# Layer 2's item (2, 6) split into high and low parts by halves in a PSUM bank, in an embedding tower on one core

## The chip, the core and the metric

The kernel runs on one core of a Trainium2 chip. The metric is the device time of one execution in microseconds, from the runs listed below. TensorE is called PE in the rows, its weight loads PEld, VectorE DVE, ScalarE ACT, GpSimd POOL and SyncE SP.

## What is computed

32 embedding tables are looked up for 1024 samples (16 numbers each), and a network of three layers works on the outcome, where each layer multiplies every field of x with every row of the last hidden state and sums with weights:

```python
for i in range(3):
    z = (x0[:, :, None, :] * h[:, None, :, :]).reshape(B, F * G, E)     # F = 32, G = 32 or 64
    y = relu(einsum('oc,bce->boe', Ws[i], z) + bs[i][None, :, None])    # 128 outputs
    x_keep, h = (y[:, :64], y[:, 64:]) if i != 2 else (y, y)
    xs.append(x_keep)
z = sum(concatenate(xs, axis=1), axis=2)
h = relu(concatenate([z, dense_ctx], axis=1) @ W_top1 + b_top1)
return relu(h @ W_top2 + b_top2) @ W_top3
```

All of it is float32. A product of a weight and an activation is made either with one float32 matmul of both (a "whole" item), or with three matmuls of a rounded type, float32r, on high and low parts: high weight by high product, low weight by high product, high weight by low product (a "split" item).

## The kernel before

**Tiles and items.** The batch has 8 blocks of 128 samples, and each block 4 tiles of 4 embedding places, so 32 tiles of 512 columns. A layer's products for one tile are cut into chunks of 128 rows, and two chunks make an item (layer, n): layer 0 has 2 items and a tail, layers 1 and 2 have 8 each. An item takes VectorE one multiplication of 128x1024 numbers (L1070): a slice of `spread` or `shifted` (the fields' rows, copied to all lanes by DMA) by the hidden state, which lies in a PSUM bank (`xT`, `h0` or `h1`).

**Slots.** The order of all work is one list written by hand (SLOT, L78), which all engines follow, each in its own order of instructions. A slot handles layer 1 of tile n, layer 2 of tile n - 1 and layer 0 of tile n + 1:

```python
SLOT = [(1, 0), (1, 1), (2, 0), (1, 2), (2, 1), (1, 3), (0, 0), (2, 2), TAIL, (1, 4), (0, 1),
        (2, 3), (1, 5), (2, 4), (1, 6), (2, 5), (1, 7), (2, 6), (2, 7)]
```

There are 34 slots, from -1 to 32. Slots 2 and up lie in a hardware loop, four to a round. The last slot has layer 2 alone.

**Whole items.** Layers 0 and 1 and item (2, 6) are whole (L101). Their products go into `prod`, a ring of 4 buffers, so VectorE waits with a product until TensorE has used the one four whole items earlier (L1067). TensorE multiplies them by w0T, w1T or w2T_whole: two chunks, each as two instructions of a float32 matmul, so four in the rows (L617).

**Split items.** The other seven of layer 2 go through three engines: VectorE writes the product (`unsplit`), ScalarE copies it to the rounded type (`high`, L829), GpSimd subtracts it from the product (`low`, L500) in the place of the product. TensorE runs four matmuls of the high part (L625) in the item's place in the list, and the two of the low part (L640) one item later. In the last slot items (2, 2), (2, 5) and (2, 7) are subtracted by VectorE (L1078).

**GpSimd.** Between its subtractions it issues the look-ups of the next block, 8 to a slot (LOOKUPS_AFTER, L95): in three slots of four one ahead of the first subtraction, then 0, 0, 1, 1, 1, 2, 2 after the seven. Of each four slots one begins a block (`begin`, L483 to L487): it waits until all look-ups of the block before have landed (s_looked) and ScalarE has copied them to `emb` (L793), takes the new indices (ids_now, L477), and goes on to look up (L490). In that slot the numbers are 0, then 0, 0, 2, 0, 1, 2, 3. The last two look-ups of a block come after the subtraction of (2, 7). ScalarE's copy to `emb` stands after its high part of (2, 2) in the slot that begins, ahead of the tail's two copies, and GpSimd's subtraction of the tail (L508) stands ahead of `begin`. Look-ups for the last block are out after slot 25, and then GpSimd only subtracts.

**ScalarE.** Besides the high parts it makes, once a slot: `next_h0` (L831), which takes layer 0's second half from y0 to the hidden state of the next tile and its first half to `kept` (three activations, after item (2, 4), as soon as TensorE has used (0, 1)); `take_x` (L805), a copy of transposed x out of xT, after (2, 5), which waits for TensorE's transposes `turn_x` (L581, L589) after (2, 4) in its own order; and, at the slot's end, `h1` (L815, L880) and the second `kept`, when TensorE has used (1, 7). The next slot's (1, 0) on TensorE waits for that `kept` (begin_layer, L601), and VectorE's (1, 0) for h0, its (2, 0) for h1. h0 has two banks, which alternate by tile.

**VectorE** also adds the kept rows (L1101; L1097 is its first in a block, a copy) after (1, 1), adds layer 2's outcome (L1114, L1109), and folds both once a block (L1120).

**SyncE** issues the loads of a slot in order: x out to HBM when take_x is done (L394), the shifted rows and four loads of 1 MB of `spread` (L416), each when VectorE has made the last product that reads the old ones: (2, 1), (2, 3), (2, 5), (2, 7).

After the last tile comes a small dense network (`three_passes`), its first layer in between the items of the last slot.

## Time and profile before

| what | value |
|---|---|
| median of 3 runs | 1061.19 us |
| the three runs | 1063.73, 1061.14, 1061.19 us |
| the profiled execution's own time | 1066.62 us |
| its span, first to last instruction | 1064.8 us |
| mean granted clock of TensorE | 0.976 |
| TensorE busy | 94% |
| VectorE busy | 77% |
| GpSimd busy | 77% |
| ScalarE busy | 45% |
| 16 DMA engines, mean rate | 174 GB/s |

The profiled execution took 5.4 us longer than the median. The rows come from it. A busy share of TensorE contains modelled ends of matmuls. The idle time in brackets at a row is that of its engine just before it, with what ended it; "issue" means that the profile shows nothing that was waited for. Weight loads run one matmul ahead of their matmul.

### The profile page before, as it was taken

The numbers are of one execution on the slowest core, as the hardware profiler recorded it, in microseconds if no ns is written. First come the engines' busy times: TensorE is split into PE (matmuls) and PEld (weight loads), VectorE is DVE, ScalarE is ACT, GpSimd is POOL, SyncE is SP. The second block draws the span as 40 slices with busy tenths as digits, with TensorE's granted clock in tenths as the row PEclk, the third lists the DMA queues.
The fourth block names the chain that finished last, engine by engine and source line by source line (L and its number), as shares of the span: only waits on it lengthen the run. The fifth ranks groups of instructions, "written<-read, shape, count | busy, mean of one in ns | idle before, by whom it ended". The sixth has DMA issues, their size and how long they took to land.

```text
span 1064.8 us, 11324 instructions
## 1 busy us (share of the span) xinstructions
PE 995.8 (94%) x3089; PEld 572.8 (54%) x3089; DVE 821.8 (77%) x750; ACT 474.4 (45%) x595; POOL 816.3 (77%) x524
## 2 busy tenths in 40 slices
PE   3178899999999999999999999999899999999988
PEld 2133455555555555555555555555455555555565
DVE  6234877798778977899778977898778977788882
ACT  2222544444544454454444454444444454543443
POOL 7655779887998879887998789886998766566540
PEclk9579999999999999999999999999999999999989
DMA  8089999989888888899888888888888888889000
GB/s 158 10 189 198 205 199 190 210 191 197 191 194 191 191 192 185 192 198 208 191 194 186 194 188 190 187 192 191 195 187 188 192 186 192 190 186 219 30 1 0
DMA packets 49012, 185.45 MB, mean 174 GB/s; under 512 B 17570, under 2 KB 22178, under 8 KB 28388
## 3 DMA queue, kind: packets, MB, share of 16 engines
q1 hardware_dynamic: 40804, 183.15, 78.2%
q0 software_dynamic: 8192, 2.11, 2.0%
q8 instruction: 7, 0.11, 0.0%
q14 instruction: 9, 0.07, 0.0%
HBM read 182.06 MB, written 3.15 MB: 174 GB/s over the span
## 4 chain that ended last, share of the span: by engine, by line
POOL 42%; PE 26%; issue 18%; DMA 7%; DVE 4%; ACT 2%; SPq 0%; POOLq 0%; ACTq 0%; DVEq 0%
POOL low L500 24%; POOL looked_up L490 16%; PE y L617 15%; PE y L625 6%; DMA looked_up<-in_tbl,ids_now 4%; PE y L640 3%; POOL tail_parts L508 2%; DMA spread<-xcols 2%; DVE unsplit L1070 1%; DVE prod L1070 1%; DMA xcols<-xrows 0%; ACT emb L793 0%; ACT tail_high L853 0%; PE y L721 0%; DVE acc_kept L1101 0%
## 5 line engine op out<-in xcount | busy, mean ns | idle before, releaser
L500 POOL TENSOR_TENSOR low<-unsplit,high 128x1024 fp32r<-128x1024 f32 x221 | 525.1, 2388 | 113.3 <-ACT high L829 111.5
L617 PE MATMUL y<-prod,w1T 128*128 128x512 f32 x1024 | 480.3, 597 | 5.4 <-ACT kept L821 2.7
L1070 DVE TENSOR_TENSOR prod<-spread,h 128x1024 f32<-128x1024 f32 x288 | 349.1, 1216 | 118.3 <-PE y L617 102.6
L829 ACT CAST high<-unsplit 128x1024 fp32r<-128x1024 f32 x224 | 234.0, 1045 | 243.6 <-DVE unsplit L1070 243.2
L1070 DVE TENSOR_TENSOR unsplit<-spread,h 128x1024 f32<-128x1024 f32 x224 | 272.1, 1215 | 48.8 <-ACT h L815 48.6
L490 POOL DMA_INDIRECT looked_up<-in_tbl,ids_now x256 | 248.7, 971 | 69.1 <-issue 59.4
L617 PEld LDWEIGHTS y<-prod,w1T 128*128 128x128 f32 x1024 | 193.5, 192 | 166.8 <-issue 144.1
L625 PE MATMUL y<-high,w2T_high 128*128 128x512 f32 x448 | 226.7, 506 | 4.4 <-ACT high L829 4.4
L640 PE MATMUL y<-low,w2T_high 128*128 128x512 f32 x448 | 202.7, 533 | 6.3 <-POOL low L500 6.3
L625 PE MATMUL y<-high,w2T_low 128*128 128x512 f32 x448 | 177.9, 397 | 0.0
L815 ACT ACTIVATE h<-y,bias 64x512 f32<-64x512 f32 x128 | 83.3, 651 | 209.2 <-PE y L617 208.3
L640 PEld LDWEIGHTS y<-low,w2T_high 128*128 128x128 f32 x448 | 84.4, 191 | 91.3 <-issue 61.5
L617 PE MATMUL y<-prod,w0T 128*128 128x512 f32 x256 | 122.2, 600 | 5.5 <-DVE prod L1070 5.5
L625 PEld LDWEIGHTS y<-high,w2T_high 128*128 128x128 f32 x448 | 84.9, 190 | 50.0 <-issue 29.4
L625 PEld LDWEIGHTS y<-high,w2T_low 128*128 128x128 f32 x448 | 84.9, 190 | 43.4 <-issue 29.0
L1070 DVE TENSOR_TENSOR prod<-shifted,xT 128x1024 f32<-128x1024 f32 x64 | 77.7, 1215 | 22.8 <-DMA shifted<-xcols 15.4
L617 PEld LDWEIGHTS y<-prod,w0T 128*128 128x128 f32 x256 | 48.9, 192 | 49.3 <-issue 45.0
L508 POOL TENSOR_TENSOR tail_parts<-tail,tail_high 128x512 fp32r<-128x512 f32 x32 | 41.0, 1283 | 25.7 <-ACT tail_high L853 25.6
L617 PE MATMUL y<-prod,w2T_whole 128*128 128x512 f32 x128 | 60.1, 592 | 0.0
L821 ACT ACTIVATE kept<-y,bias_kept 64x512 f32<-64x512 f32 x64 | 43.7, 682 | 1.6
L809 ACT COPY xrows<-xT 48x512 f32<-48x512 f32 x32 | 18.5, 579 | 50.6 <-PE xT L589 50.6
L589 PE MATMUL xT<-ident,four_times 128*128 128x128 f32 x128 | 20.2, 282 | 22.2 <-ACT four_times L801 22.2
(115 smaller groups left out, 441.3 us busy)
## 6 DMA issues: line engine op xcount, KB each, us to landing
spread<-xcols SPq DMA_DIRECT2D x128, 1024.0 KB, 9.0
shifted<-xcols SPq DMA_DIRECT2D x124, 256.0 KB
shifted_tail<-xcols SPq DMA_DIRECT2D x124, 64.0 KB
looked_up<-in_tbl,ids_now POOLq DMA_INDIRECT x256
xcols<-xrows SPq DMA_DIRECT2D x32, 96.0 KB, 2.0
spread<-in_L_rec_W SPq DMA_DIRECT2D x3, 512.0 KB, 7.0
spread<-in_L_rec_W SPq DMA_DIRECT2D x1, 1024.0 KB, 11.6
wt<-in_W_top SPq DMA_DIRECT2D x2, 512.0 KB, 8.7
```

What stands on the lines that cost most here:

```text
L490: pool.indirect_dma_start(out=looked_up[:, f, :], out_offset=None, in_=tables[f][:, :], in_offset=bass.IndirectOffsetOnAxis(ap=ids_now[:, ...
L500: pool.tensor_tensor(low[kind][r][:, :, :], unsplit[kind][r][:, :, :], high[kind][r][:, :, :].bitcast(F32), ALU.subtract).then_inc(s_low[k ...
L508: pool.tensor_tensor(tail_parts[:, :], tail[:, :], tail_high[:, :].bitcast(F32), ALU.subtract).then_inc(s_tail_low, 1)
L589: last = pe.transpose(xT[:, P * e:P * (e + 1)], four_times[:, e, :, :].rearrange("p a f -> p (a f)"), ident[:, :])
L617: last = pe.matmul(y[:, :], w, z[:, c, :], start=(n == 0 and c == 0), stop=(item in (LAST0, LAST1) and c == ITEM - 1))
L625: pe.matmul(y[:, :], w[:, ITEM * n + c, :], z[:, c, :], start=(n == 0 and c == 0 and w is w2T_high), stop=False)
L640: last = pe.matmul(accumulator(s, layer)[:, :], w2T_high[:, ITEM * n + c, :], z[:, c, :], start=False, stop=(item == LAST2 and c == ITEM - 1))
L809: act.copy(xrows[:, :], xT[0:XROWS, :]).then_inc(s_xrows, 1)
L815: last = act.activation(h[to, :], y[lanes, :], ACT.Relu, bias=bias[lanes, :])
L821: act.activation(kept[t[1] % KEPT][lanes, :], y[lanes, :], ACT.Relu, bias=bias_kept[lanes, :]).then_inc(s_kept, 1)
L829: act.copy(high[kind][r][:, :, :], unsplit[kind][r][:, :, :]).then_inc(s_high[kind], 1)
L1070: dve.tensor_tensor(z, x[:, ITEM * n:ITEM * (n + 1), :], b[:, :].unsqueeze(1).to_broadcast([P, ITEM, COLS]), ALU.mult).then_inc(s_made[kin ...
```

## The change

Item (2, 6) is no longer whole. In the last slot it is split like the others, with GpSimd's subtraction, and the order there is as before. In all other slots that have layer 2 it is split with VectorE's, chunk by chunk in one PSUM bank, `part`, and without a place in `unsplit`: VectorE writes the product of a chunk to the bank (`make_part`), ScalarE copies it from there to the high part (`part_high`), VectorE subtracts the high part from the bank into the low part (`part_low`), and only then makes the second chunk there. The bank is taken from h0, which has one bank instead of two, so `next_h0` also waits until VectorE has made (1, 7), the last product that reads the old h0, and moves from behind (2, 4) to behind (1, 7) in ScalarE's order. VectorE and ScalarE follow a new list with the last items in another order (MADE), while TensorE, GpSimd and SyncE keep SLOT. The ring `prod` keeps 4 buffers and holds ten items a slot instead of eleven. `w2T_whole` and its copy are gone.

```diff
+MADE = SLOT[:-4] + [(2, 6), (2, 5), (1, 7), (2, 7)]
-WHOLE2 = (2, 6)
+IN_PARTS = (2, 6)
 def kind_of(item, last):
-    if item[0] < 2 or item == WHOLE2:
+    if item[0] < 2:
         return WHOLE
-    return BY_DVE if last and item in LAST_BY_DVE else BY_POOL
+    return BY_DVE if item in (LAST_BY_DVE if last else [IN_PARTS]) else BY_POOL
+def made_items(items):
+    return [x for x in MADE if x in items] if IN_PARTS in items and (1, 7) in items else items
-        w2T_whole = sb("w2T_whole", [P, ITEM, P])
-        h0 = [ps(f"h0_{p}", [P, COLS]) for p in range(2)]
+        h0 = ps("h0", [P, COLS])
+        part = ps("part", [P, COLS])
...
+            def part_high(s, c):
+                e = plan.entry(s, IN_PARTS)
+                act.wait_ge((s_part, s_made[BY_DVE])[c], e + 1)
+                to = high[BY_DVE][plan.place(s, IN_PARTS, RING)]
+                act.copy(to[:, c, :], part[:, :]).then_inc((s_part_high, s_high[BY_DVE])[c], 1)
             def next_h0(s):
                 act.wait_ge(s_used[WHOLE], plan.entry(s, LAST0) + 1)
-                go_on(h0[(s[1] + 1) % 2], y0, 1, bias0, s_h0)
+                if LAST1 in plan.items(s):
+                    act.wait_ge(s_made[WHOLE], plan.entry(s, LAST1) + 1)
+                go_on(h0, y0, 1, bias0, s_h0)
...
-                h0_after = (2, 4) if (2, 4) in items else None
+                h0_after = (1, 7) if (2, 4) in items else None
-                for item in items:
+                last_slot = plan.is_last(s)
+                for item in made_items(items):
...
+                    elif item == IN_PARTS and not last_slot:
+                        part_high(s, 0)
                     elif plan.kind(s, item) != WHOLE:
+                        if item == LAST2 and not last_slot:
+                            part_high(s, 1)
                         split_high(s, item)
...
-                    if WHOLE2[1] // (GROUP // ITEM) == n - 2 - GROUPS:
-                        of = ITEM * WHOLE2[1] % GROUP
-                        dve.tensor_copy(w2T_whole[:, :, :], source[:, of:of + ITEM, :])
...
+            def make_part(s, c):
+                e = plan.entry(s, IN_PARTS)
+                if c == 0 and (not isinstance(e, int) or e >= RING[BY_DVE]):
+                    dve.wait_ge(s_used[BY_DVE], e - RING[BY_DVE] + 1)
+                if c == 1:
+                    dve.wait_ge(s_part_low, e + 1)
+                elif not isinstance(e, int) or e >= 1:
+                    dve.wait_ge(s_low[BY_DVE], e)
+                dve.tensor_tensor(part[:, :], spread[(s[1] - 1) % 2][:, ITEM * IN_PARTS[1] + c, :], h1[:, :],
+                                  ALU.mult).then_inc((s_part, s_made[BY_DVE])[c], 1)
+            def part_low(s, c):
+                e = plan.entry(s, IN_PARTS)
+                dve.wait_ge((s_part_high, s_high[BY_DVE])[c], e + 1)
+                r = plan.place(s, IN_PARTS, RING)
+                dve.tensor_tensor(low[BY_DVE][r][:, c, :], part[:, :], high[BY_DVE][r][:, c, :].bitcast(F32),
+                                  ALU.subtract).then_inc((s_part_low, s_low[BY_DVE])[c], 1)
...
             def slot(s):
                 waiting = None
                 items = plan.items(s)
-                for item in items:
-                    mine = item != TAIL and plan.kind(s, item) == BY_DVE
-                    multiply(s, item)
-
+                in_parts = IN_PARTS in items and not plan.is_last(s)
+                for item in made_items(items):
+                    whole_item = not (in_parts and item == IN_PARTS)
+                    mine = item != TAIL and whole_item and plan.kind(s, item) == BY_DVE
+                    if whole_item:
+                        multiply(s, item)
+                    else:
+                        make_part(s, 0)
+
+                    if in_parts and item == (2, 5):
+                        part_low(s, 0)
+                    if in_parts and item == LAST1:
+                        make_part(s, 1)
+                    if in_parts and item == LAST2:
+                        part_low(s, 1)
```

## Rows read from the trace of the kernel before

**Rows 1.** Page, busy us (share of the span) xinstructions of three engines

```profile
PE 995.8 (94%) x3089; PEld 572.8 (54%) x3089; DVE 821.8 (77%) x750; ACT 474.4 (45%) x595; POOL 816.3 (77%) x524
```

**Rows 2.** Busy time by stretch: us, PE, PEld, DVE, ACT, POOL, PEclk, DMA share, GB/s

```profile
200.00:900.00 700.00, 696.70 (x2160) 399.06 (x2159) 579.22 (x509) 331.08 (x409) 591.46 (x369) 1.00 0.88 192
```

**Rows 3.** Timeline of weight loads, slots at 573 and 602, and one late load

```profile
573.13 0.42 PEld L617 LDWEIGHTS y<-prod,w1T 128*128 128x128 f32 x2
579.01 0.19 PEld L640 LDWEIGHTS y<-low,w2T_high 128*128 128x128 f32 x1 [0.24 <-issue]
602.45 0.42 PEld L617 LDWEIGHTS y<-prod,w1T 128*128 128x128 f32 x2
...
520.68 0.30 PEld L640 LDWEIGHTS y<-low,w2T_high 128*128 128x128 f32 x2 [1.00 <-POOL low L500]
```

**Rows 4.** Page, chain of work that ended last, share of the span by engine

```profile
POOL 42%; PE 26%; issue 18%; DMA 7%; DVE 4%; ACT 2%; SPq 0%; POOLq 0%; ACTq 0%; DVEq 0%
```

**Rows 5.** Chain of work late on: start us, us, what; items (2, 6) and (2, 7)

```profile
955.78 1.72 PE y L617 x4
957.50 0.93 PE y L625 x4
```

**Rows 6.** Timeline of VectorE, slot that starts at 573.13

```profile
568.00 3.38 DVE L1101 TENSOR_TENSOR acc_kept<-acc_kept,kept 128x512 f32<-128x512 f32 x1
...
579.19 0.67 DVE L1052 TENSOR_TENSOR tail<-shifted_tail,xT 128x512 f32<-128x512 f32 x1
579.79 1.21 DVE L1070 TENSOR_TENSOR prod<-spread,h 128x1024 f32<-128x1024 f32 x1
...
588.20 1.21 DVE L1070 TENSOR_TENSOR unsplit<-spread,h 128x1024 f32<-128x1024 f32 x1
...
597.32 3.12 DVE L1097 COPY acc_kept<-kept 128x512 f32<-128x512 f32 x1
```

**Rows 7.** Timeline of GpSimd: start us, us, engine, line, operation [idle before]

```profile
510.99 2.36 POOL L500 TENSOR_TENSOR low<-unsplit,high 128x1024 fp32r<-128x1024 f32 x1
518.24 7.06 POOL L500 TENSOR_TENSOR low<-unsplit,high 128x1024 fp32r<-128x1024 f32 x3
...
593.03 2.38 POOL L500 TENSOR_TENSOR low<-unsplit,high 128x1024 fp32r<-128x1024 f32 x1 [1.59 <-ACT high L829]
597.77 2.37 POOL L500 TENSOR_TENSOR low<-unsplit,high 128x1024 fp32r<-128x1024 f32 x1
614.60 0.21 POOL L477 COPY ids_now<-ids_sb 128x32 int32 x1
```

**Rows 8.** Timeline of ScalarE in the slot that starts at 573.13

```profile
589.99 1.32 ACT L815 ACTIVATE h<-y,bias 64x512 f32<-64x512 f32 x2 [2.73 <-PE y L617]
591.91 1.03 ACT L829 CAST high<-unsplit 128x1024 fp32r<-128x1024 f32 x1
594.54 0.58 ACT L809 COPY xrows<-xT 48x512 f32<-48x512 f32 x1 [1.59 <-PE xT L589]
595.02 1.04 ACT L829 CAST high<-unsplit 128x1024 fp32r<-128x1024 f32 x1
599.30 1.31 ACT L815 ACTIVATE h<-y,bias 64x512 f32<-64x512 f32 x2 [3.24 <-PE y L617]
```

**Rows 9.** Chain of work in the middle: start us, us, what

```profile
497.04 0.22 POOL ids_now L477
...
601.58 8.66 DMA looked_up<-in_tbl,ids_now
```

**Rows 10.** Waits of the weight loads up to 200 us: us in total, times, longest

```profile
PEld xT L589 <- ACT four_times L801: 22.6, 1, 22.6
```

**Rows 11.** Timeline of GpSimd where its loop of slots ends

```profile
744.01 0.96 POOL L490 DMA_INDIRECT looked_up<-in_tbl,ids_now  x1 [3.80 <-issue]
```

**Rows 12.** Timeline of VectorE in the last slot

```profile
1026.71 2.43 DVE L1147 TENSOR_TENSOR z_kept_low<-z_kept,z_high 128x512 fp32r<-128x512 f32 x1
1031.34 0.68 DVE L1155 TENSOR_TENSOR hidden_low<-hidden,hidden_high 128x512 fp32r<-128x512 f32 x1
```

13 lines of the change are left out of this document (8 added, 5 removed).

## The prediction

> **What bounds the kernel now.** I read the page's busy times first: TensorE is at 94% of the span, VectorE and GpSimd at 77% each [rows 1]. The table by stretch sharpens that: from 200 to 900 us TensorE is busy for 696.7 of 700 us at the full granted clock [rows 2]. The weight loads give the period of a slot: item (1, 0) starts at 573.13 and again at 602.45, so 29.32 us [rows 3]. So TensorE's own work sets the pace, and a shorter item shortens the slot. But the page's chain of work that ended last runs through GpSimd for 42% of the span and through TensorE for 26% [rows 4]. That is the warning: in each block there is a long unbroken run of GpSimd, and its end shows at one weight load, which comes 1.00 us after the last in place of the usual 0.24, waiting for a low part [rows 3]. GpSimd is barely in time there.
>
> I write A for the slot that starts at 573.13, B for the next (602.45), C for the one after, and "A+20" for a time 20 us into A.
>
> **TensorE's gain.** The whole item is four instructions in 1.72 us, the four of a split item's high part 0.93 us, so 0.2325 each [rows 5]. Split, (2, 6) takes six: 6 x 0.2325 = 1.40. Gain 0.32 us a slot, 29.32 to 29.00, in 32 slots at most 10.2 us (1.0%). The Trainium skill, "TensorE: Matmul & The Clock Gate", Back-to-back issue gap, gives 131 ns for a matmul of 512 columns in a stream with weight loads. By it six take 0.79 us and the gain would be 0.93 a slot; the trace has 232 ns, and the measurement decides.
>
> **VectorE's added work.** One multiplication of 128x1024 goes and four operations of 128x512 come. The tail's product, with one operand in PSUM, is such a one: 0.67 us, the next starts after 0.60 [rows 6]. A 1024 multiplication has 1.21 us, so by the same overlap a pitch of about 1.13. So 4 x 0.60 - 1.13 = +1.3 us a slot. No row has VectorE writing PSUM. I take the tail's 0.60; the bounds are 0.3 less (half the tail's) and that of the worst VectorE row of this size, 3.38 us [rows 6]. VectorE is busy for 579.2 of 700 us [rows 2], so idle for 5.1 us in a slot, and its time itself is hidden. If that cover were gone, 1.3 us a slot would be 42 us. `part_low` reads one operand from PSUM, and this decides whether it meets GpSimd: additions with both operands in SBUF take 0.68 alone [rows 12] and 3.38 or, a copy, 3.12 us when a GpSimd subtraction runs [rows 6, 7], while multiplications from PSUM keep 1.21 beside it. The Trainium skill, "SBUF — State Buffer", Who interferes with whom, says a VectorE instruction with at most one SBUF input does not contend with GpSimd; by it `part_low` stays at 0.6, and from two SBUF operands it would be up to 3. The trace agrees for multiplications; no row has a subtraction of this kind.
>
> **ScalarE's order is the costly part.** Before, `next_h0` ran at A+16.9 (589.99), between the high parts of (2, 4) and (2, 5); then (2, 5) at 591.91, `take_x` at 594.54, which waits for TensorE's transposes, then (2, 7) at 595.02 [rows 8]. Now `take_x` comes before `next_h0`, which stands behind (1, 7). So after A+21.4, ScalarE does in one run: take_x 0.48, h0 1.34, kept 0.58, second half of (2, 6) about 0.5 (take_x's own pitch), high part of (2, 7) 1.05. Done at A+25.4, before A+22.9. Three things stand behind it:
> - h1 starts at A+26.2 (599.30) when (1, 7) is done, as before [rows 8]; 0.7 us are left.
> - VectorE's second `part_low` is at A+24.4, and behind it in VectorE's order (1, 0), (1, 1), the addition and (2, 0). (1, 0) is made at A+26.2, needed at A+29.0. The addition falls on A+27.3, onto GpSimd's low part of (2, 7), and ends about A+28.5; (2, 0) is made at A+29.7 and its high part at 30.8. TensorE wants it after (1, 0) and (1, 1), at A+29.0+3.4=32.4. Hidden, with 1.6 us left. In A, which has two folds, VectorE ran from 571.4 (568.00 + 3.38, A-1.7) without a pause; now it starts at about A-0.2, so it makes (2, 5) from A+17.2 in place of A+15.1 (588.20) plus the first half [rows 6]; (1, 7) at A+20.2 is before A+21.9, where h0 needs it.
> - GpSimd's low part of (2, 7). It started at A+24.64 (597.77), after the two look-ups behind (2, 5) (593.03) [rows 7]. Now it can't before A+25.5: **+0.85 us**.
>
> **What that 0.85 meets.** Behind that low part come a block's last two look-ups; the last lands and reaches ScalarE 8.66 us after it is issued [rows 9], then emb, the tail and the new block's indices at B+12.15 (614.60) [rows 7]. Relative to B this moves by 0.85 + 0.32 to B+13.3. From there GpSimd has no pause: from the like point of the block before, 497.04, it ends the low part of (2, 7) at 513.35 (16.3 later) and of the next (2, 0) at 520.6 (23.6 later) [rows 7, 9]. Now:
> - (2, 7)'s low part ends at B+29.6. TensorE wants it 0.47 us before the slot's end, with its load 0.23 earlier at most, B+28.5: stall 1.1 us.
> - (2, 0)'s, at B+36.9. C starts at B+30.1, wants it at C+5.88 (579.01 - 573.13) [rows 3], B+36.0; a load runs some 0.3 ahead there, so 0.6 more.
> Before, the same sum gives 35.8 + 0 against 29.32 + 5.88 = 35.2, less 0.3: a stall of 0.3, which is the late load of the rows. So a block of four slots takes 4 x 29.32 + 0.3 = 117.6 now (614.60 - 497.04 = 117.56 [rows 7, 9]) and 4 x 29.00 + 1.7 = 117.7 after. **GpSimd's run takes back the gain** in the six blocks' time in which look-ups are issued: 6 x 0.15 = +0.9 us. The stall of 3.80 us in one issue where GpSimd's loop ends [rows 11] stays as it is; it is in the same run.
>
> **Without look-ups**, from about 780 us on, nine items (2, 6) gain in full: -2.9 us.
>
> **Start.** w2T_whole's copy goes from VectorE's preparation: TensorE's first transposes wait 22.6 us for the first look-ups after that [rows 10], so 0. ScalarE's `next_h0` in slot 0 may wait for (1, 7): up to +0.5, taken as 0.
>
> **End.** Slot 31 has VectorE in one run with extra subtractions of the dense network, so the added 1.3 us are not fully hidden; in the last slot the item's low part comes to GpSimd at 1031.4, where VectorE has a subtraction out of SBUF at 1031.34 that takes 0.68 [rows 12], and such a one takes 2.43 when it meets GpSimd. Bounds: -0.3 (the PE time alone) and 1.3 + 1.75 = +3.0; I take +1.0, below the middle, since TensorE still has a unit of the dense layer to do meanwhile.
>
> **Sum.** 0.9 - 2.9 + 0 + 1.0 = -1.0 us on the profiled execution's own 1066.6 (span 1064.8 and 1.8 around it): 1065.6. The median stands 5.4 lower, so 1060.2. A measurement tells about 0.3% (3.2 us) from no change.
>
> **Rivals.**
> 1. *GpSimd has more room than the profile shows; the gain comes through.* For: the timed runs are 5.4 us shorter, and TensorE's work can't be what shrank from 200 to 900 us, so part of that may be GpSimd's issue and the look-ups' landing. If the run of 40 us from (2, 7)'s low part in A to (2, 0)'s in C is 1.7 us shorter, no stall is left: -10.2 + 0.3 x 6 for what the faster run of before also saves there, + 1.0 at the end: about -8, 1053. At half of it, 1057. Against: GpSimd's subtractions have 2.36 to 2.38 us wherever they stand [rows 7], so they show no disturbance.
> 2. *The last look-up lands later: slower.* The DMA engines are at 88% [rows 2]; SyncE's megabyte loads are issued at the same time as a block's last two look-ups, and these now come 0.85 us later among them. Each microsecond beyond 8.66 goes into the run uncovered, six times. It decides from 0.7 us on: six times 0.7 - 1.0 = +3.2. With 1.5 us: +8, 1069. Against: the megabyte loads are out in any case by then, and a look-up is small beside them.
> 3. *VectorE and ScalarE take turns badly.* A write to the bank at twice the tail's time, or a wait of each of the four steps of 0.1 us, moves (2, 7)'s high part, thus +0.5 a block and 0 elsewhere: +3, 1064.
> 4. *The change does not do what it says:* accesses of `part` beside TensorE's banks hold TensorE, or the six matmuls don't run at 0.2325. Nothing in the rows is for it: 1061 to 1064.
>
> **Chances.** Forecast 45%; rival 1, 35%; rival 2, 10%; rivals 3 and 4, 5% each. Faster by over 0.3%: 0.36 (rival 1 and a little of the forecast); same 0.47; slower 0.17. The range takes in the forecast with its end at both bounds (1059 to 1063), rival 1 whole, and the near part of 2 and 3: 1052.5 to 1065.5.
>
> **What the changed profile would show.** Distance of (1, 0)s 29.00 where nothing waits; TensorE's gaps before (2, 7)'s and (2, 0)'s low part of 1.1 and 0.6 us in one slot pair of four; `next_h0` at A+21.9 and (2, 7)'s high part ending at A+25.4; `part` operations on VectorE of about 0.67. Wrong would be: those gaps gone while GpSimd's indices are at B+13.3 or sooner; high parts later than A+26; TensorE waiting for (2, 0)'s high part or for ScalarE's kept.

## The result, and the profile after

| what | before | after |
|---|---|---|
| median | 1063.73 us of 7 | 1054.62 us of 7 |
| range | 1061.14 to 1065.91 | 1053.63 to 1056.56 |
| profiled execution's own time | 1066.62 | 1055.05 |
| its span | 1064.8 | 1053.2 |

The ratio is 0.9925 [0.9913, 0.9938]: faster by 0.75%, 8.0 us. (The two medians of the table are 9.1 us apart; the ratio with its interval is the figure used here.) The forecast was 1060.2, 1.0 us below the kernel before, and "within 0.3%" as its likeliest case. What came is close to rival 1, the gain comes through, with its 1053. The difference of the two profiled spans, 11.6 us, is larger than the ratio says: before's profiled execution took longer than any of its seven timed ones.

Page of the changed kernel, busy times and the chain that ended last:

```profile
PE 987.6 (94%) x3153; PEld 585.1 (56%) x3153; DVE 829.3 (79%) x842; ACT 511.2 (49%) x658; POOL 823.2 (78%) x525
PE 61%; POOL 17%; issue 8%; DMA 5%; DVE 5%; ACT 2%; SPq 0%; POOLq 0%; DVEq 0%; ACTq 0%
```

Against [rows 1], TensorE has 64 matmuls more (each whole item had four, a split one has six) and 8.2 us less to do. VectorE has 92 instructions more and 7.5 us more busy time, ScalarE 63 and 36.8 us. The chain, which ran through GpSimd for 42% and TensorE for 26% [rows 4], now has 17% and 61%. Most of what GpSimd held in it is TensorE's now.

Table by stretch, 200 to 900 us, columns as in [rows 2]:

```profile
200.00:900.00 700.00, 698.21 (x2234) 412.94 (x2233) 587.72 (x590) 363.40 (x463) 601.71 (x373) 1.00 0.89 195
```

TensorE rose from 696.7 to 698.2 of 700 us at the full granted clock, though each slot has less work for it: waits have gone, not come. The forecast wanted the opposite, 1.7 us of wait in four slots in place of 0.3, so some 8 us less than before in this stretch (six blocks by 1.4).

Timeline of weight loads, start of slots A (568.27) and B (597.30), the transposes of `turn_x` in A (588.75), and the one late load in the slot after B:

```profile
568.27 0.43 PEld L627 LDWEIGHTS y<-prod,w1T 128*128 128x128 f32 x2
588.75 0.38 PEld L599 LDWEIGHTS xT<-ident,four_times 128*128 128x128 f32 x2
597.30 0.42 PEld L627 LDWEIGHTS y<-prod,w1T 128*128 128x128 f32 x2
632.81 0.30 PEld L650 LDWEIGHTS y<-low,w2T_high 128*128 128x128 f32 x2 [0.86 <-POOL low L510]
```

From 568.27 to 597.30 are 29.03 us, and over many slots 29.01: the 29.00 of the forecast. Of the two late loads that it wanted in each block there is one, before the low part of (2, 0), with 0.86 us in place of the usual 0.24. It makes that slot 29.33, by 0.32 longer than the others. Before, the same load came late as well [rows 3], and the slot was longer by 0.29 to 0.45.

Timeline of ScalarE over the end of A and the start of B:

```profile
589.69 0.58 ACT L819 COPY xrows<-xT 48x512 f32<-48x512 f32 x1 [2.31 <-PE xT L599]
590.30 1.32 ACT L825 ACTIVATE h<-y,bias 64x512 f32<-64x512 f32 x2
591.64 0.69 ACT L831 ACTIVATE kept<-y,bias_kept 64x512 f32<-64x512 f32 x1
592.22 0.57 ACT L846 CAST high<-part 128x512 fp32r<-128x512 f32 x1
592.69 1.05 ACT L839 CAST high<-unsplit 128x1024 fp32r<-128x1024 f32 x1
594.45 1.31 ACT L825 ACTIVATE h<-y,bias 64x512 f32<-64x512 f32 x2 [0.72 <-PE y L627]
603.32 1.05 ACT L839 CAST high<-unsplit 128x1024 fp32r<-128x1024 f32 x1 [2.35 <-DVE unsplit L1091]
604.27 0.61 ACT L803 COPY emb<-looked_up 128x512 f32<-128x512 f32 x1
```

This is the order that the forecast worked out: `take_x` at A+21.4 (589.69 - 568.27 = 21.42), h0 at A+22.0 where A+21.9 was forecast, part_high 0.57 where 0.5 was, and the high part of (2, 7) done at A+25.47 where A+25.4 was. The last two rows are what was not worked out. `emb` is copied at 604.27 right behind the high part of (2, 2), which had waited for VectorE's product; there is no wait for a DMA. Before, ScalarE was done with that high part and then waited 1.5 us for the look-ups.

Timeline of GpSimd from (2, 7)'s low part in A to the three subtractions ahead of the late load:

```profile
593.82 2.40 POOL L510 TENSOR_TENSOR low<-unsplit,high 128x1024 fp32r<-128x1024 f32 x1 [1.31 <-ACT high L839]
596.36 0.97 POOL L500 DMA_INDIRECT looked_up<-in_tbl,ids_now  x1
597.63 0.94 POOL L500 DMA_INDIRECT looked_up<-in_tbl,ids_now  x1 [0.31 <-issue]
...
608.62 0.21 POOL L487 COPY ids_now<-ids_sb 128x32 int32 x1
...
622.83 2.39 POOL L510 TENSOR_TENSOR low<-unsplit,high 128x1024 fp32r<-128x1024 f32 x1 [0.32 <-ACT high L839]
...
630.37 4.76 POOL L510 TENSOR_TENSOR low<-unsplit,high 128x1024 fp32r<-128x1024 f32 x2
```

(2, 7)'s low part starts at A+25.55, where "not before A+25.5" was forecast; the step of +0.85 us is there, and the row names ScalarE's high part as what ended 1.31 us of idle time. But the new indices (608.62) are at B+11.32. The forecast had B+13.3; before it was B+12.15 [rows 7]. This is where the forecast and the chip part.

Timeline of VectorE in A, then the groups of the two new operations (min/median/max in ns):

```profile
592.82 0.69 DVE L1112 TENSOR_TENSOR low<-part,high 128x512 fp32r<-128x512 f32 x1 [3.08 <-ACT high L846]
593.53 2.35 DVE L1091 TENSOR_TENSOR prod<-spread,h 128x1024 f32<-128x1024 f32 x2
595.80 0.70 DVE L1139 COPY acc_kept<-kept 128x512 f32<-128x512 f32 x1
596.42 1.21 DVE L1091 TENSOR_TENSOR unsplit<-spread,h 128x1024 f32<-128x1024 f32 x1
L1104 DVE TENSOR_TENSOR part<-spread,h x62: 675/683/690, 116.8 to 996.1; 128x512 f32<-128x512 f32 x62
L1112 DVE TENSOR_TENSOR low<-part,high x62: 672/684/693, 118.5 to 997.8; 128x512 fp32r<-128x512 f32 x62
```

The operations in `part` take 0.683 and 0.684 us (0.67 forecast), and in 62 cases each never over 0.693, whether the bank is the destination or an operand. A subtraction of GpSimd runs beside 60 of the products and beside 23 of VectorE's subtractions, and none of these is over 0.690. The copy of the kept rows took 3.12 us on top of GpSimd's low part before [rows 6]. The forecast had it at A+27.3, on the end of that low part, and done at about A+28.5. It starts at A+27.53 with 0.4 us of GpSimd's subtraction still to go (593.82 + 2.40 = 596.22) and takes 0.70.

The Trainium skill, "SBUF — State Buffer", Who interferes with whom, says that a VectorE instruction with at most one input in SBUF, outside the two-port modes, does not contend with GpSimd. The trace agrees for `part_low` too (at most 0.683 us in the 23 beside a GpSimd subtraction), which the trace of before could not show.

Waits from 200 to 900 us, us in total, times, longest:

```profile
PEld y L650 <- POOL low L510: 6.4, 6, 1.5
DVE low L1112 <- ACT high L846: 111.4, 24, 5.4
ACT xrows L819 <- PE xT L599: 93.3, 24, 4.6
ACT emb L803 <- DMA looked_up<-in_tbl,ids_now: 0.5, 1, 0.5
```

TensorE's waits for a low part were 16.7 us in the same view of before, 42 times; 6.4 us in 6 waits are left. VectorE idles for 111.4 us before the subtraction of a half, all of it hidden. ScalarE's wait for a looked-up row was 8.8 us, six times, up to 1.7; it is 0.5, once.

**Where the time went**, by the distances between the transposes from slot 3 to slot 31 in the two profiled executions. Before: 28 slots of 29.32 are 821.0 us, and 7.7 more in stalls. After: 28 of 29.01 are 812.3, and 5.2 in stalls. So TensorE's shorter slot gives 8.7 us, and stalls 2.5. All of the 2.5 is one place, the slot in which GpSimd's loop ends: 33.25 us before (3.9 over), 30.35 after (1.3 over). There GpSimd pauses ahead of one look-up, for 3.80 us before [rows 11] and 1.48 after. From the last slot's transposes to the end it is 115.1 before and 114.6 after, where the forecast added 1.0.

### The profile page after: what moved, and what is told of

Read it like the earlier page. It is cut to its first block, busy times and chain, and to the rows that moved or that the text cites. A ratio compares the mean times of both kernels' runs of the same rounds, so it can differ in the third digit from the quotient of the medians.

```text
span 1053.2 us, 11585 instructions
## 1 busy us (share of the span) xinstructions
PE 987.6 (94%) x3153; PEld 585.1 (56%) x3153; DVE 829.3 (79%) x842; ACT 511.2 (49%) x658; POOL 823.2 (78%) x525
## 4 chain that ended last, share of the span: by engine, by line
PE 61%; POOL 17%; issue 8%; DMA 5%; DVE 5%; ACT 2%; SPq 0%; POOLq 0%; DVEq 0%; ACTq 0%
PE y L627 36%; PE y L635 15%; POOL looked_up L500 8%; POOL low L510 8%; PE y L650 8%; DMA xcols<-xrows 2%; DMA shifted<-xcols 2%; DVE unsplit L1091 2%; DVE prod L1091 1%; PE xT L599 1%; DMA looked_up<-in_tbl,ids_now 1%; PE y L644 1%; SPq L411 0%; POOL tail_parts L518 0%; ACT h L825 0%
## 5 line engine op out<-in xcount | busy, mean ns | idle before, releaser
L1091 DVE TENSOR_TENSOR prod<-spread,h 128x1024 f32<-128x1024 f32 x256 | 306.6, 1209 | 16.0 <-ACT h L825 9.6
L635 PE MATMUL y<-high,w2T_high 128*128 128x512 f32 x512 | 240.3, 469 | 4.6 <-ACT high L839 4.6
L650 PE MATMUL y<-low,w2T_high 128*128 128x512 f32 x512 | 218.5, 516 | 3.1 <-POOL low L510 2.8
L635 PE MATMUL y<-high,w2T_low 128*128 128x512 f32 x512 | 203.0, 396 | 0.0
L1112 DVE TENSOR_TENSOR low<-part,high 128x512 fp32r<-128x512 f32 x62 | 42.5, 685 | 133.0 <-ACT high L846 133.0
L650 PEld LDWEIGHTS y<-low,w2T_high 128*128 128x128 f32 x512 | 96.3, 190 | 90.6 <-issue 71.3
L635 PEld LDWEIGHTS y<-high,w2T_high 128*128 128x128 f32 x512 | 96.9, 189 | 47.5 <-issue 19.6
L635 PEld LDWEIGHTS y<-high,w2T_low 128*128 128x128 f32 x512 | 96.7, 189 | 40.6 <-issue 22.0
L1091 DVE TENSOR_TENSOR prod<-shifted,xT 128x1024 f32<-128x1024 f32 x64 | 77.4, 1209 | 17.1 <-DMA shifted<-xcols 15.9
L518 POOL TENSOR_TENSOR tail_parts<-tail,tail_high 128x512 fp32r<-128x512 f32 x32 | 41.0, 1280 | 15.9 <-ACT tail_high L873 15.9
L846 ACT CAST high<-part 128x512 fp32r<-128x512 f32 x62 | 35.8, 577 | 33.9 <-DVE part L1104 33.9
```

Source lines behind the costliest of these rows:

```text
L518: pool.tensor_tensor(tail_parts[:, :], tail[:, :], tail_high[:, :].bitcast(F32), ALU.subtract).then_inc(s_tail_low, 1)
L635: pe.matmul(y[:, :], w[:, ITEM * n + c, :], z[:, c, :], start=(n == 0 and c == 0 and w is w2T_high), stop=False)
L650: last = pe.matmul(accumulator(s, layer)[:, :], w2T_high[:, ITEM * n + c, :], z[:, c, :], start=False, stop=(item == LAST2 and c == ITEM - 1))
L846: act.copy(to[:, c, :], part[:, :]).then_inc((s_part_high, s_high[BY_DVE])[c], 1)
L1091: dve.tensor_tensor(z, x[:, ITEM * n:ITEM * (n + 1), :], b[:, :].unsqueeze(1).to_broadcast([P, ITEM, COLS]), ALU.mult).then_inc(s_made[kin ...
L1112: dve.tensor_tensor(low[BY_DVE][r][:, c, :], part[:, :], high[BY_DVE][r][:, c, :].bitcast(F32), ALU.subtract).then_inc((s_part_low, s_low[ ...
```

## Why the indices come earlier

The forecast took over the 8.66 us from a block's last look-up to `emb` [rows 9]. In the changed kernel it is 604.27 - 597.63 = 6.64, and in the blocks before and after it 6.63. These 6.6 us are not the look-up's own time: ScalarE has no wait for it there, so they only tell when ScalarE gets to `emb`, B+6.97, where it was B+7.81 before. The packets of the look-ups' queue tell when the look-ups landed. I compare two stretches of 4 us in each kernel, from 9 to 13 us behind the transposes (which are at 588.75 after and 593.6 before) and from 13 to 17. DMA view of the changed kernel, 597.7 to 601.7 us (in the next stretch it has none):

```profile
q0 software_dynamic: 64, 0.02, 2.3%
```

The same of the kernel before, 602.6 to 606.6 and 606.6 to 610.6 us:

```profile
q0 software_dynamic: 32, 0.01, 1.2%
q0 software_dynamic: 32, 0.01, 1.8%
```

Each look-up is 32 packets. Before, the last two land one by one, the second in the later stretch; after, both land in the first, in spite of being issued 0.9 us later against the transposes. SyncE's issues, changed kernel first:

```profile
586.32 0.54 SPq L426 DMA_DIRECT2D spread<-xcols  x1
590.48 0.36 SPq L404 DMA_DIRECT2D xcols<-xrows  x1
593.86 1.87 SPq L411 DMA_DIRECT2D shifted<-xcols  x4
598.02 2.44 SPq L426 DMA_DIRECT2D spread<-xcols  x2
```

and before:

```profile
589.43 0.54 SPq L416 DMA_DIRECT2D spread<-xcols  x1
595.33 0.36 SPq L394 DMA_DIRECT2D xcols<-xrows  x1
597.32 1.88 SPq L401 DMA_DIRECT2D shifted<-xcols  x4
601.48 15.96 SPq L416 DMA_DIRECT2D spread<-xcols  x4
```

Both kernels write x out 1.7 us behind the transposes. The load ahead of it, the third megabyte of `spread`, is issued 4.2 us before them in the old kernel and 2.4 in the new one, since VectorE now makes the first half of (2, 6) ahead of (2, 5), and that load waits for (2, 5). x's way out queues behind it: the shifted rows, which wait for x, go out at +3.7 before and +5.1 after, and the next megabyte at +7.9 and +9.3. So the two look-ups (at +6.7 and +8.0 before, +7.6 and +8.9 after) now are both issued ahead of that megabyte; before, the second came behind it. How much that order is worth can be read from all 14 traces of this case, the experiments below among them, in five blocks of each (those whose `emb` comes after 250 us): how long behind the last look-up SyncE issues the next megabyte, and how long behind it the look-up's last packet is done.

| next megabyte issued | blocks | last packet done |
|---|---|---|
| from 0.5 us ahead of the last look-up to 0.17 behind it | 24 | 5.85 to 8.0 us behind the look-up |
| 0.21 us or more behind the last look-up | 46 | 3.35 to 5.3 us behind the look-up |

No block is an exception, and several kernels have blocks in both rows. The changed kernel has one in the first, at 371.79 (0.16 us, done after 6.3, a wait of 0.5), and so has its repetition e11, here in a timeline of GpSimd, SyncE (716 to 719 us) and ScalarE:

```profile
717.10 0.94 POOL L500 DMA_INDIRECT looked_up<-in_tbl,ids_now  x1 [0.30 <-issue]
717.13 0.58 SPq L426 DMA_DIRECT2D spread<-xcols  x1
725.54 0.62 ACT L803 COPY emb<-looked_up 128x512 f32<-128x512 f32 x1 [1.72 <-DMA looked_up<-in_tbl,ids_now]
```

The megabyte is 0.03 us behind the look-up there, the packets are done after 7.65, and `emb` comes 8.44 us behind it, as in the kernel before. So a look-up issued 0.2 us or more ahead of the megabyte lands some 3 us sooner. What follows for `emb` is less than these 3 us, because ScalarE's high part of (2, 2) then comes last: it is at most the wait for the look-up, 1.5 us in the block shown.

## The experiments

Each ran beside the kernel before on the same chip, and ratios are to that one. This table puts together what the weight loads and GpSimd's index copies of each profile say: a slot's distance where nothing waits, how much longer the slot with the late load is in the blocks of slots 12 to 23, and the place of the new indices behind the start of slot B (slot 20, or the one a block earlier).

| kernel | ratio | slot | stall per block | indices | in the loop's last slot |
|---|---|---|---|---|---|
| before | 1 | 29.32 | 0.29, 0.45, 0.29 | 12.15 | 3.9 |
| after | 0.9925 | 29.01 | 0.64, 0.32, 0.32 | 11.3 | 1.3 |
| e11, the same again | 0.9931 | 29.01 | 0.32, 0.32, 0.33 | 11.3 | 1.9 |
| e1 | 0.9996 | 29.31 | 0 | 11.7 | 1.7 |
| e2 | 1.0021 | 29.32 | 0.6, 0.7, 0.6 | 12.2 | 4.4 |
| e3 | 1.0025 | 29.01 | 2.4, 2.4, 2.4 | 12.9 | 6.0 |
| e4 | 1.0057 | 29.49 | 0.3, 0.5, 0.1 | 11.9 | 0.8 |
| e5 | 0.9935 | 29.01 | 0.4, 0.9, 0.4 | 11.4 | 2.2 |
| e6 | 0.9932 | 29.01 | 0.41, 0.37, 0.40 | 11.3 | 1.6 |
| e7 | 0.9850 | 28.55 | 1.5, 1.4, 1.1 | 12.0 | 3.1 |
| e8 | 0.9905 | 29.01 | 0.1, 0, 0 | 10.8 | 1.3 |
| e9 | 1.0000 | 29.01 | 2.1, 2.1, 2.1 | 12.6 | 3.6 |
| e10 | 1.0002 | 29.01 | 1.6, 1.5, 1.6 | 11.4 (first of five) | 6.7 |
| e12, e8 again | 0.9912 | 29.01 | 0.1, 0, 0 | 11.0 | 1.7 |

### e1: only the third load, later (kernel before)

```diff
-                    item = (2, GROUP // ITEM * (g + 1) - 1)
+                    item = WHOLE2 if g == 2 else (2, GROUP // ITEM * (g + 1) - 1)
```

> The kernel before, with one thing changed: SyncE issues the third of the four loads of spread in a slot when VectorE has made (2, 6), not (2, 5), about 1.8 us later. Theory L (the block's last look-up lands sooner in the changed kernel because the third load, now issued later, pushes x's way out to HBM and the fourth load back, so that the last two look-ups are served ahead of that load): the last look-up reaches ScalarE 7 us or less after its issue in place of 8.7, the new block's indices come about 1.5 us earlier in the slot, the late low part once a block (0.3 us) goes, and the time falls by 1 to 4 us. Rival (the look-ups land sooner because they are issued 0.9 us later themselves): landing stays 8.7 us, the time is that of before within 0.1%.

1062.93 us, ratio 0.9996 [0.9985, 1.0007]: no change. The stall of 0.3 us in a block is gone, and the look-ups' packets have all moved by 12.5 us behind the transposes (12.2 to 12.9 in four of the changed kernel's five blocks, 15.1 to 15.9 before). So moving the third load alone, and with it the next, makes the look-ups land sooner. But `emb` comes at 8.2 to 8.5 us behind the last look-up all the same, where 7 or less was expected; that expectation failed. VectorE's waits show why:

```profile
DVE prod L1070 <- DMA shifted<-xcols: 16.9, 21, 2.6
```

In this kernel VectorE is there before the shifted rows and waits for them, 21 times, so the high part of (2, 2), behind which ScalarE has `emb`, comes later itself. In the changed kernel VectorE has that wait once, for 0.7 us. So the early landing isn't enough: it takes effect in the changed kernel because VectorE there hardly waits for those rows. And with TensorE's old slot there were only the 0.3 us a block to be had, which is below what the comparison can tell.

### e2: only ScalarE's order and the one bank (kernel before)

```diff
-        h0 = [ps(f"h0_{p}", [P, COLS]) for p in range(2)]
+        h0 = ps("h0", [P, COLS])
...
+                if LAST1 in plan.items(s):
+                    act.wait_ge(s_made[WHOLE], plan.entry(s, LAST1) + 1)
+                go_on(h0, y0, 1, bias0, s_h0)
...
-                h0_after = (2, 4) if (2, 4) in items else None
+                h0_after = (1, 7) if (2, 4) in items else None
```

> The kernel before with one bank for h0 and next_h0 behind (1, 7), item (2, 6) whole as before. Theory T (only TensorE's shorter item gives time): the slot stays 29.32 us where nothing waits, the time is that of before within 0.3%; the high part of (2, 7) ends at A+24.9, the low part of (2, 7) starts there instead of at A+24.6. Rival (the single bank and the order cost something that the shorter item hides in the changed kernel): 0.3% or more slower, by the look-ups' run: up to six times 1 us. A second rival (the order itself gives part of the gain, by better turns of the DMA queues): faster by 1 to 3 us.

1065.43, ratio 1.0021 [1.0012, 1.0029]. The order with the single bank costs 2.2 us, with stalls of 0.6 to 0.8 a block. Here the last look-up still takes 8.4 to 8.7 us to `emb`, so the later high part is handed on as the forecast said. The next megabyte is issued ahead of the last look-up in all five blocks, by 0.05 to 0.5 us.

### e3: the item split, with its product in SBUF as one piece (kernel before)

```diff
-    if item[0] < 2 or item == WHOLE2:
+    if item[0] < 2:
         return WHOLE
-    return BY_DVE if last and item in LAST_BY_DVE else BY_POOL
+    return BY_DVE if item in (LAST_BY_DVE if last else [WHOLE2]) else BY_POOL
```

(and `w2T_whole` left out).

> The kernel before, with (2, 6) split by VectorE in the ordinary way: product of 128x1024 to SBUF, high part by ScalarE, subtraction out of SBUF by VectorE; two banks for h0 and the old order; w2T_whole gone. TensorE does what it does in the changed kernel. Theory P (the PSUM bank matters, since a subtraction with both operands in SBUF waits for GpSimd's): the subtraction takes about 1.2 us alone and up to 3.5 beside GpSimd, VectorE's busy time rises by 50 us or more, some of it reaches TensorE or GpSimd, and the time lies between the two kernels, 1056 to 1061. Rival (VectorE has room enough, the bank gives nothing): the time of the changed kernel, 1054 to 1055, or below it, as h0 keeps its early place.

1065.55, ratio 1.0025 [1.0015, 1.0035]. TensorE has the same instructions as in the changed kernel and the same slot of 29.01, and nothing of the gain comes through; the 1056 to 1061 that were expected did not come. It is the forecast's own mechanism, and more strongly than it had it. Of this kernel a VectorE row, two of GpSimd, and TensorE's wait from 200 to 900 us (before 16.7, changed 6.4):

```profile
507.81 2.59 DVE L1074 TENSOR_TENSOR low<-unsplit,high 128x1024 fp32r<-128x1024 f32 x1 [4.58 <-ACT high L828]
```
```profile
509.46 1.77 POOL L489 DMA_INDIRECT looked_up<-in_tbl,ids_now  x1 [0.16 <-issue]
515.05 1.24 POOL L489 DMA_INDIRECT looked_up<-in_tbl,ids_now  x1 [0.16 <-issue]
```
```profile
PEld y L639 <- POOL low L499: 23.7, 35, 2.6
```

VectorE's subtraction out of SBUF lies on GpSimd's at 506.91 and takes 2.59 us instead of 1.23; the look-up that GpSimd issues meanwhile takes 1.77 us instead of 0.96. The stall adds up from two terms. The indices come at B+12.88 in place of 11.32, 1.56 later, and from the indices to the three subtractions GpSimd needs 22.32 us (497.73 to 520.05) in place of 21.75 (608.62 to 630.37), 0.57 more. Together 2.13; the slots are longer by 2.44 and 0.32, which differ by 2.12. The first term is the look-ups' landing, for ScalarE waits for them in each block of e3 (200 to 900 us; 8.8 us before, 0.5 in the changed kernel):

```profile
ACT emb L792 <- DMA looked_up<-in_tbl,ids_now: 11.5, 6, 2.1
```

The second is mostly the stretched issue, 0.81 us, less the 0.33 us for which GpSimd in the changed kernel waits for ScalarE.

### e4: two more matmuls in the item (changed kernel)

The added product, of low weights and low products, is not in the reference's arithmetic as the kernel splits it.

```diff
+                if item == IN_PARTS:
+                    for c in range(ITEM):
+                        pe.matmul(accumulator(s, layer)[:, :], w2T_low[:, ITEM * n + c, :], z[:, c, :],
+                                  start=False, stop=False)
```

> The changed kernel, where (2, 6) gets two more matmuls (low weight by low product, so eight in place of six). Theory T (TensorE's work sets the slot): 2 x 0.2325 = 0.46 us more a slot, 29.01 to 29.48, in 32 slots +14.8 us: 1069, 0.5% over the kernel before. Rival (GpSimd's run sets the block, TensorE has slack): a part of it only, +3 to +8 us.

1068.37, ratio 1.0057 [1.0044, 1.0071]. The slot grows by 0.48 us, and the time by 1.32% against the changed kernel's 0.9925, 14.0 us; 31 times 0.48 are 14.9. TensorE's work sets the slot of the changed kernel in full.

### e5: the halves in SBUF (changed kernel)

```diff
-                dve.tensor_tensor(part[:, :], spread[...], h1[:, :],
+                to = unsplit[BY_DVE][plan.place(s, IN_PARTS, RING)][:, c, :]
+                dve.tensor_tensor(to, spread[...], h1[:, :],
...
-                dve.tensor_tensor(low[BY_DVE][r][:, c, :], part[:, :], high[BY_DVE][r][:, c, :].bitcast(F32),
+                dve.tensor_tensor(low[BY_DVE][r][:, c, :], unsplit[BY_DVE][r][:, c, :], high[BY_DVE][r][:, c, :].bitcast(F32),
```

> The changed kernel with the halves of (2, 6) in SBUF instead of the PSUM bank: VectorE writes each half's product into the item's own buffer, ScalarE reads it there, VectorE subtracts there (both operands in SBUF). Orders, waits and the single h0 bank as changed. Theory P (PSUM keeps the subtraction out of GpSimd's way): some subtractions take 2 to 3 us in place of 0.68 and GpSimd's look-ups or low parts beside them take longer; time 1 to 4 us over the changed kernel's. Rival (the order of VectorE's work and with it of the loads gives all, the bank nothing): 1054 to 1055, and no subtraction over 1 us that matters.

1056.95, ratio 0.9935 [0.9921, 0.9948]. The group of the subtraction, min/median/max in ns:

```profile
L1113 DVE TENSOR_TENSOR low<-unsplit,high x62: 680/693/4603, 117.4 to 999.2; 128x512 fp32r<-128x512 f32 x62
```

Out of SBUF up to 4.6 us against 0.693 at most out of PSUM. The 23 subtractions that have one of GpSimd's beside them take 0.94 to 4.6 us, the 39 others at most 0.73. So the bank does what it is there for. The time rises by 0.1% (0.9925 to 0.9935), within the intervals, as VectorE has the idle time for it. So what e3 lost is not the operand's place by itself. What is left between e3 and e5 is the halves, with the order of VectorE's and ScalarE's work that comes with them, and so the order of the loads: e5's last look-up is issued ahead of the next megabyte in all five blocks, by 0.16 to 1.6 us, e3's in none.

### e6 and e10: more work in GpSimd's run (changed kernel)

```diff
-                pool.tensor_copy(ids_now[:, :], ids_sb[:, bass.ds(b, 1), :]).then_inc(s_now, 1)
+                for again in range(2):
+                    pool.tensor_copy(ids_now[:, :], ids_sb[:, bass.ds(b, 1), :]).then_inc(s_now, 1)
```

e10 has range(5).

> The changed kernel, where GpSimd copies a block's indices twice, each time waiting for the copy, at the begin of each block: 1.1 us more in its run. Theory R (GpSimd's run after a new block's indices has no room, as its 0.3 us stall per block says): TensorE's stall for the low parts rises from 0.3 to about 1.4 us a block, time +6 to +7 us. Rival (the run has room, the gain of TensorE is what the time follows): +0 to +2 us.

> The changed kernel with the block's indices copied five times in place of once: e6 showed 0.38 us for one more copy and 0.33 us of room before the low part of (2, 7), so four more are 1.5 us, 1.2 beyond that room. Theory R (GpSimd's run is what the stall comes from): stall for (2, 0)'s low part in C and for (2, 7)'s in B together 1.4 to 1.6 us a block in place of 0.3, time +6 to +8 us against the changed kernel. Rival: there is more room, +0 to +3 us.

e6: 1056.50, ratio 0.9932 [0.9918, 0.9945]. A copy more is only 0.38 us (492.13 to 492.50), so the dose missed and the expected 6 to 7 us could not come. It still tells something small: GpSimd idles for 0.32 us before (2, 7)'s low part (622.83 above), 0.38 - 0.32 are 0.06, and the stalls are 0.37 to 0.41 in place of 0.32. e10: 1068.09, ratio 1.0002 [0.9992, 1.0012], against 0.9931 of e11 on the same chip 0.71%, 7.6 us. Its five copies start at 502.83, 503.20, 503.57, 503.95 and 504.33, so the four added ones are 1.50 us. Less the room of 0.32 and plus the stall of 0.32 that was there, that makes a stall of 1.50; 1.53 to 1.64 were measured, and 1.4 to 1.6 expected. TensorE's wait from 200 to 900 us, few and long:

```profile
PEld y L651 <- POOL low L511: 17.8, 13, 3.3
```

So the run behind the indices has no more than 0.32 us of room; it starts sooner. And that room lies ahead of (2, 7)'s low part, where GpSimd waits for ScalarE's high part at B+25.5: the indices could come up to 0.3 us later, or sooner by any amount, and the late load would not move. The stall of 0.32 us that is left is counted from that high part.

### e7: two matmuls fewer (changed kernel)

```diff
-                        for w in (w2T_high, w2T_low):
+                        for w in (w2T_high,) if item == IN_PARTS else (w2T_high, w2T_low):
```

It leaves out the product of low weights and high products for item (2, 6).

> The changed kernel, where TensorE leaves out the two matmuls of low weight by high product of (2, 6): 0.46 us less a slot. Theory T (TensorE's work alone): slot 28.55, -14.8 us: about 1040. Rival R (GpSimd's run takes back part): slots 28.55 in between, but each block's stall grows from 0.3 by about 0.46 for each slot between the new indices and the late low part, 0.5 to 0.9 us a block; time -9 to -12 us.

1048.38, ratio 0.9850 [0.9836, 0.9864]. The slot is 28.55, 0.46 less, 14.3 us in 31 slots; the time falls by 0.75% more than the changed kernel's, 8.0 us, where 9 to 12 were expected with GpSimd's run taking part and 14.8 without. Stalls of 1.0 to 1.5 us a block are back (0.5 to 0.9 expected), and the loop's last slot has 3.1 over in place of 1.3:

```profile
PEld y L650 <- POOL low L510: 20.3, 46, 2.2
```

The next shortening of TensorE's slot is about half taken back by GpSimd's run. The forecast's mechanism is right as a mechanism, one step of shortening further on.

### e8 and e12: `take_x` behind (2, 7) (changed kernel)

```diff
-                x_after = (2, 5) if (2, 5) in items else None
+                x_after = (2, 7) if (2, 5) in items else None
```

> The changed kernel, where ScalarE's take_x (the copy of transposed x, which waits for TensorE) stands behind the high part of (2, 7) instead of behind that of (2, 5), so that h0, the second half of (2, 6) and (2, 7) don't wait for TensorE's transposes. Theory R (the high part of (2, 7) behind take_x makes GpSimd's run late): low part of (2, 7) starts at A+22 to A+24.6 in place of A+25.5, the last look-ups come as much earlier, the 0.3 us stall a block goes, VectorE's 111 us of waiting for part_high mostly goes, time -1 to -2.5 us. Rival (the load of x goes out later and with it the spread loads, DMA being busy for 88%): VectorE waits for shifted or spread, same or slower by 1 to 3 us.

> The kernel of e8 again, beside the changed kernel on one chip: no late low part once a block (0.3 us in five blocks) and so 0.5 to 2.5 us faster than the changed kernel if its stalls were all that differs; equal if e8's lead was chance.

e8: 1053.79, ratio 0.9905 [0.9890, 0.9920]; e12: 1058.76, 0.9912 [0.9898, 0.9926], beside e11's 0.9931 on the same chip. Timeline of ScalarE and two waits from 200 to 900 us in e8:

```profile
585.94 1.31 ACT L825 ACTIVATE h<-y,bias 64x512 f32<-64x512 f32 x2 [0.68 <-DVE prod L1091]
588.33 1.05 ACT L839 CAST high<-unsplit 128x1024 fp32r<-128x1024 f32 x1
589.28 0.58 ACT L819 COPY xrows<-xT 48x512 f32<-48x512 f32 x1
```
```profile
DVE low L1112 <- ACT high L846: 20.3, 24, 1.2
DVE unsplit L1091 <- ACT h L825: 87.0, 24, 4.5
```

The second half and (2, 7) no longer stand behind the transposes, which come late. The high part of (2, 7) starts 0.9 us behind the start of the transposes (588.33 - 587.5) in place of 3.9 (592.69 - 588.75), the indices are at B+10.8, and the stall in a block is gone. VectorE waits for h1 instead, hidden. Both ratios are 0.2% below the changed kernel's, 2 us, as far as the stalls of 0.3 in six blocks go. The intervals overlap, so this is the best version measured, but by a step that two comparisons only suggest.

### e9: e3 with the third load later

The edits of e3 and of e1 together.

> The kernel of e3 (ordinary split of (2, 6) by VectorE in SBUF, two h0 banks, old order), with e1's later third load of spread on top. e3 had stalls of 2.4 us a block: 0.3 as before, 0.6 from two shorter slots, 0.6 from the new block's indices at B+12.9, 1.1 from look-ups held up beside VectorE's subtraction. Theory L (the look-ups' landing, and with it the moment of the indices, is what separates e3 from the changed kernel, beside the 1.1): indices at B+11.5 to B+12.3, stalls of 1.0 to 1.8 us a block, time 4 to 8 us under e3's. Rival (it is the collision of the subtraction alone): stalls stay over 2 us and the time within 2 us of e3's.

1067.84, ratio 1.0000 [0.9991, 1.0009], 0.25% or 2.7 us below e3, where 4 to 8 were expected. The indices come at B+12.6, only 0.3 earlier than in e3, and the look-up held up by VectorE is there too (1.77 us). The look-ups land sooner, with their last packet 4.1 to 4.6 us behind the issue in place of 7.7 to 8.0, and ScalarE no longer waits for them. But VectorE waits for the shifted rows here as in e1 (10.1 us, six times), and so ScalarE's high part of (2, 2) is late itself. So the load's place alone doesn't bring the 1.5 us.

### e11: the changed kernel again

> The changed kernel itself, beside e12 and the kernel before on one chip. All theories: 1054 to 1055, ratio 0.992 to 0.993. Its profile tells which of the differences between two profiled executions are the execution's: the stall where GpSimd's loop of slots ends should be 1.3 us again if it comes from the later loads, anything from 1 to 4 us if it is chance.

1059.88, ratio 0.9931 [0.9918, 0.9944], with stalls of 0.32, the indices at B+11.3 and 6.63 us from the last look-up to `emb` in three blocks; the block at 725.54 shown above has its indices at B+13.15. In the loop's last slot it has 1.9 us over where 1.3 was expected, but without GpSimd's pause of 1.48 us, so that pause is not the same from one execution to the next. The result holds on another chip.

## Why the prediction came out as it did

The time lay in the range only because the range took rival 1 in. The forecast's own case was a change of -1.0 us, 1060.2; the measured one is -8.0, at a median 5.6 us below that, and the mechanism that the forecast held likeliest, GpSimd's run takes back the gain, is not what happened. By the forecast's own steps:

- **TensorE's gain**, 29.32 to 29.00: 29.01, and e4 and e7 move with it. The trace's 232 ns a matmul was the right price. The Trainium skill, "TensorE: Matmul & The Clock Gate", Back-to-back issue gap, has 131 ns; worked out from that figure, as an estimate, the slot would have been 28.4.
- **VectorE**, +1.3 us hidden, 0.67 an operation out of PSUM: 0.683, hidden.
- **ScalarE's order**, each time within 0.15 us. The step from it, "**+0.85 us**" on GpSimd's low part of (2, 7): there, at A+25.55.
- **"What that 0.85 meets"** is the step that failed, in the sentence "Relative to B this moves by 0.85 + 0.32 to B+13.3". It takes the 8.66 us from the last look-up to `emb` as fixed. These 8.66 us held a wait of 1.5 us for a look-up behind a megabyte load, and the change moved the loads: 6.63 measured, no wait, and B+11.32. The run behind the indices was mis-sized by less: 24.2 us to the load (B+35.5 less B+11.3; 632.81 - 608.62 = 24.2) where 23.6 was taken. Of these 0.6 us, 0.32 are GpSimd's wait for ScalarE's high part of (2, 7) in B: the forecast had worked out for A that the low part can't start before A+25.5, and didn't apply it to B. Another 0.27 are one look-up's issue behind that low part, 1.23 us at 625.38 where the like one before took 0.97. The sum goes through with these: 1.7 us forecast, less 1.98 for the indices, plus 0.6 for the run, are 0.3; measured 0.32. Of the two late loads, that before (2, 7)'s low part is gone, that before (2, 0)'s is left.
- The addition, at A+27.3 and done at A+28.5: A+27.53 to A+28.23.
- **The loop's end**, "stays as it is": it didn't. Less the stall that every block has, that slot has 3.6 us over before, 3.8 in e2 and 3.6 in e3, whose loads go out as before. In the kernels whose third load goes out later it is about 0.5 to 1.7 (the last column less the mean of the stalls), in all of them but e10, with 5.1. It goes with GpSimd's own pause in that slot: 3.55 to 3.80 us before and in e2, e3 and e10, 1.35 to 2.16 in the others; e11 has none, and its 1.9 us are what indices 1.8 us late give (less the room of 0.3, plus the stall of 0.3). In e10 the indices were 1.1 us late on top of the pause. So the loads' place may have a part in the pause, but e10, whose third load goes out later, has the long one too, and what sets it is not shown. How far the timed executions share in it is open: e1's profile has 2.2 us less of it than before's, and its median moved by 0.4.
- **The end**, +1.0: -0.5 in the profiled executions.
- **Rival 1** gave 1053 (its terms, -10.2 + 1.8 + 1.0, add up to -7.4, so 1053.8) and was half right. It asked for GpSimd's run of 40 us, from (2, 7)'s low part in A to (2, 0)'s in C, to be 1.7 us shorter, and named the look-ups' landing as a place. That run is 38.9 us (593.82 to 632.7) where it was 40.4, so 1.5 shorter. But its reason, that the timed executions are shorter than the profiled one, is not what did it: the change moved the loads. And behind the indices, as e6 and e10 show, there is 0.3 us of room.
- **Rival 2**, the look-up lands later: the right place with the wrong sign. It named the megabyte loads that the look-ups meet, and took those as fixed in time, but VectorE's new order moved them by more (1.4 us) than it moved the look-ups (0.9).

What stays open: why 0.2 us of lead decides when a look-up lands, and what sets the pause at the loop's end. No experiment moves the loads in the changed kernel back; that they matter there rests on e1, on the blocks on both sides in one kernel, and on the sum above. How the 8.0 us of the timed executions divide between the shorter slot and the loop's end is known for the profiled executions alone.

## What to carry to other kernels

A latency read off the trace of before holds only as long as its queue neighbours keep their places. Where a step ends in a DMA of a few packets behind megabyte loads, work out where each of those loads moves too, before adding a delay of its issue to its landing. And ask what would come last if it landed sooner: here that was VectorE's and ScalarE's work on (2, 2), so that the last packet came 3.3 us earlier in the slot (B+7.0 before, B+3.7 after) but `emb` only 0.84 (B+7.81, B+6.97). When a bound engine's work is cut, look for the engine with no room over a whole period, and expect the next cut to be taken back by it: here 8.0 of 9.6 us (31 slots by 0.31) came through, and of the next 14.3 again 8.0.

## What was not expected of the hardware

- When a look-up's 32 packets move depends on 0.2 us in the order of issue. With the next megabyte load issued 0.17 us behind it or earlier, its last packet was done 5.85 to 8.0 us after its issue (24 blocks); with the load 0.21 us or more behind it, 3.35 to 5.3 (46 blocks). In the blocks shown it was 7.9 us before (601.58, load at 601.48) and 3.4 in the changed kernel (597.63, load at 598.02).
- VectorE's products into PSUM took at most 690 ns beside a GpSimd subtraction (60 cases) and its subtractions with one operand in PSUM at most 683 (23 cases); with both operands in SBUF these took 941 to 4603 ns beside one, and at most 732 elsewhere (e5). It also stretched GpSimd's issue of a look-up from 0.96 to 1.77 us (e3).
- The same kernel before has medians of 1063.3, 1064.3 and 1067.6 us on three chips, so 0.4% between chips, more than most of the steps studied here. Each ratio above compares runs on one chip.
